# A vision tower on one core: gamma folded into a second out product, residual with row sums by VectorE, rests of B and C by TensorE, a third unit times B by GpSimd, steps re-placed

## What is computed

```
h = h + attn(layernorm(h))
attn(x):
    x_inner, z = split(x @ W_in)                      # 384 channels each
    x_conv = silu(conv4(x_inner) + conv_b)
    B, C  = split(x_conv @ W_x)                       # 16 states each
    delta = softplus(x_conv @ W_dt + b_dt)
    for t: s = exp(delta[t] * A) * s + delta[t] * x_conv[t] * B[t]
           y[t] = sum over states of s * C[t]
    y = (y + D * x_conv) * silu(z)
    out = y @ W_out
    return (out - mean(out)) / sqrt(var(out) + 1e-5) * gamma + beta
ffn: h = h + experts(layernorm(h))                    # router on layernorm(h), capacity, top 1
```

## Time and profile before

| | |
|---|---|
| median of 3 runs | 2686.87 us (2685.8 to 2687.75) |
| the profiled execution, its own time | 2688.49 us |
| span of its instructions | 2686.8 us |
| PE busy / weight loads | 2361.2 us (88%) / 1497.1 us |
| DVE busy | 2228.8 us (83%) |
| POOL busy | 2162.1 us (80%) |
| ACT busy | 2058.0 us (77%) |

### The profile page before, as it was taken

How to read it: one execution, slowest core, us unless ns; L and a number is a source line. 1 busy time by engine, 2 the same in 40 slices (tenths; PEclk the granted TensorE clock), 3 DMA queues, 4 the chain that set the end, 5 groups by cost and what they waited for, 6 DMA issues and landing times. The chain is left out here.

```text
span 2686.8 us, 37764 instructions
## 1 busy us (share of the span) xinstructions
PE 2361.2 (88%) x12483; PEld 1497.1 (56%) x12483; DVE 2228.8 (83%) x2304; ACT 2058.0 (77%) x4606; POOL 2162.1 (80%) x1004
## 2 busy tenths in 40 slices
PE   7798898988989988988989898998885479999997
PEld 4444555545555554555555455555442278888887
DVE  1799999999999999999999999999999885222222
ACT  2789988899999999899889999999986463333333
POOL 0599999999999999999999999999998314544432
PEclk9999999999999999999999999999986589999999
DMA  3445555555555555555555555555443035766654
GB/s 110 115 122 135 132 131 120 118 131 138 130 124 118 118 118 135 122 133 130 135 119 119 136 132 132 122 118 118 118 112 87 19 109 190 232 222 220 218 182 156
DMA packets 164569, 361.07 MB, mean 134 GB/s; under 512 B 17457, under 2 KB 88697, under 8 KB 156952
## 3 DMA queue, kind: packets, MB, share of 16 engines
q1 hardware_dynamic: 152504, 329.59, 48.6%
q0 software_dynamic: 11872, 29.07, 3.3%
HBM read 292.28 MB, written 68.52 MB: 134 GB/s over the span
## 5 line engine op out<-in xcount | busy, mean ns | idle before, releaser
L1600 DVE TENSOR_TENSOR_SCAN arena<-banks,arena 128x788 f32<-128x788 f32 x768 | 1339.9, 1778 | 1.4 <-ACT banks L733 1.0
L541 POOL TENSOR_TENSOR arena<-arena 128x1576 f32<-128x1576 f32 x384 | 1242.6, 3260 | 23.7 <-DVE arena L1600 22.9
L733 ACT ACTIVATE banks<-arena,neg_a 128x392 f32<-128x392 f32 x1536 | 839.1, 580 | 95.2 <-DVE arena L1600 84.6
L1589 DVE TENSOR_TENSOR arena<-arena,banks 128x1576 f32<-128x1576 f32 x320 | 565.7, 1768 | 24.5 <-PE banks L1130 14.5
L1146 PE MATMUL banks<-arena,gather_q 128*32 128x394 f32 x3072 | 341.8, 526 | 22.5 <-POOL arena L541 21.7
L1093 PE MATMUL banks<-arena,v_lo 128*128 128x394 f32 x768 | 293.2, 526 | 8.9 <-ACT arena L816 8.0
L1852 DVE TENSOR_TENSOR arena<-banks,arena 128x384 f32<-128x384 f32 (+1 forms) x57 | 30.2, 530 | 325.4 <-PE banks L1471 325.4
L693 POOL DMA_INDIRECT out_tokens<-arena x106 | 107.2, 1011 | 231.0 <-DVE arena L1867 207.3
L1072 PE MATMUL banks<-wtok,arena 128*99 128x192 f32 x1536 | 264.5, 329 | 13.9 <-DMA arena<-in_x 11.5
L1072 PEld LDWEIGHTS banks<-wtok,arena 128*99 128x99 f32 x1536 | 249.3, 167 | 35.9 <-issue 30.3
L1040 ACT ACTIVATE arena<-banks 128x256 f32<-128x256 f32 (+1 forms) x57 | 21.1, 370 | 281.9 <-PE banks L1437 281.9
(11 more groups left out here) (272 smaller groups left out, 4103.2 us busy)
## 6 DMA issues: line engine op xcount, KB each, us to landing
arena<-delta_du_scratch SPq DMA_DIRECT2D x384, 394.0 KB, 10.6
arena<-in_w_pack SPq DMA_DIRECT2D x57, 1155.0 KB, 5.3
delta_du_scratch<-arena SPq DMA_DIRECT2D x96, 394.0 KB, 3.5
arena<-in_x SPq DMA_DIRECT2D x32, 1176.0 KB, 10.5
rows_scratch<-arena SPq DMA_DIRECT2D x32, 297.0 KB
rows_scratch<-arena SPq DMA_DIRECT2D x32, 294.0 KB
arena<-in_b SPq DMA_DIRECT2D x57, 96.0 KB, 5.2
arena<-in_conv_w SPq DMA_DIRECT2D x1, 2304.0 KB, 11.0
```

What stands on the lines that cost most here:

```text
L541: pool.tensor_tensor(v[:, :, :], v[:, :, :], c_rep[(NG * n + u % NG) % CREPS].unsqueeze(1).to_broadcast([P, NQ, N2]), ALU.mult).then_inc(s ...
L733: ins = act.activation(o, d, ACT.Exp, scale=neg_a[:, c:c + 1])
L1589: dve.tensor_tensor(hb[(UNITS * n + u) % BUFS][:, :, :], rep[m][:, :, 1, :], ps_b[:, 0:N2].unsqueeze(1).to_broadcast([P, NQ, N2]), ALU.mul ...
L1600: dve.tensor_tensor_scan(v, decay[k % 2], v, 0.0, ALU.mult, ALU.add).then_inc(s_scan, 1)
```

## The change

1. **Gamma in a second out product.** `wog` is the centred out weights times gamma, made once by VectorE. `scaled_product` multiplies y by it; `out_product` stays, but only its squares are used, and ScalarE takes them straight from the bank (`out_squares`, now by halves b). `copy_out`, `out_norm` and `apply_gamma` go.
2. **Residual by VectorE.** `add_residual` (two halves of two instructions) computes bank x 1/deviation + (h + beta) and sums each row; ScalarE makes mean and squares of the rows (`row_squares`) in place of VectorE's statistics.
3. **Rests of B and C by TensorE.** `less_first` and `less_second` add minus identity times the bf16 part to the bank of the product; ScalarE copies the second and third part from that bank. `rest_bc` and `last_bc` go.
4. **Unit 1's product with B by GpSimd**: `BY_POOL = (1, 5, 9)`.
5. **Other places** for steps on all four engines, other bank numbers. Both token halves now use banks of one parity (`TOKS` 9 and 11), both halves of the front transposes do not (`FT` 19 and 20). In the last passes the two residual steps stand ahead of `weigh` and `choose` on VectorE.

```diff
-        BY_POOL = (5, 9)
+        BY_POOL = (1, 5, 9)
...
-        K_OF = (20, 1, 21, 12, 8, 7, 4, 15, 13, 14)
-        OUT, TOKS, FT = (5, 6), (9, 10), (17, 19)
-        BT, CS, ROUTE = (11, 16), (22, 0, 2, 3), 18
+        K_OF = (22, 1, 23, 21, 8, 5, 4, 16, 6, 14)
+        OUT, TOKS, FT = (2, 10), (9, 11), (19, 20)
+        BT, CS, ROUTE = (12, 15), (24, 0, 3, 7), 18
+        OUTG = (13, 17)
...
+            def out_squares(n, r, o, b):
+                act.wait_ge(s_opmm, 2 * n + b + 1)
...
+                for f in range(2):
+                    c = 2 * b + f
+                    ins = act.activation(rows[r][:, c, DIM:2 * DIM], kbank(OUT[b], o)[0:H0, f * DIM:(f + 1) * DIM], ACT.Square,
+                                         accum_out=sq2[:, c:c + 1])
+                ins.then_inc(s_osq, 1)
...
+            def less_first(n, r, o):
+                pe.wait_ge(s_gev, 10 * n + TAKEN[BC])
+                pe.matmul(kbank(K_OF[BC], o)[:, 0:N2], minus, bc3[r], start=False, stop=True,
+                          skip_group_check=True).then_inc(s_bcrest, 1)
...
+            def scaled_product(n, o, b):
...
+                v = kbank(OUTG[b], o)
+                for f in range(2):
+                    c = b * L + f * HSTEP
+                    for k in range(MB):
+                        mm = pe.matmul(v[0:H0, f * DIM:(f + 1) * DIM], y[:, k, c:c + H0], wog[:, k, :], start=(k == 0),
+                                       stop=(k == MB - 1))
+                mm.then_inc(s_ogmm, 1)
...
+            def add_residual(n, r, o, b):
+                dve.wait_ge(s_ogmm, 2 * n + b + 1)
...
+                for f in range(2):
+                    c = 2 * b + f
+                    ins = dve.scalar_tensor_tensor(out=rows[r][:, c, 0:DIM], in0=kbank(OUTG[b], o)[0:H0, f * DIM:(f + 1) * DIM],
+                                                   scalar=rs2[:, c:c + 1], in1=rows[r][:, c, 0:DIM], op0=ALU.mult, op1=ALU.add,
+                                                   accum_out=sum3[:, c:c + 1])
+                ins.then_inc(s_resid, 1)
...
+                    if 2 in on and u == 5:
+                        pe.wait_ge(s_h, 2 * (i + 2) + 1)
+                        tok(i + 2, r, 1)
...
+                    if 2 in on and u == 6:
+                        if -1 in on:
+                            pe.wait_ge(s_resid, 2 * (i - 1) + 2)
+                        else:
+                            pe.wait_ge(s_h, 2 * (i + 2) + 2)
+                        front_t(i + 2, r, 0)
```

More of the change, by code:

```diff
@@ L164, in build @@
         h2_hi = carve(P, 4, H0)
-        st1, st3 = (carve(H0, 4, 6) for _ in range(2))
-        mv1, mv3 = (carve(H0, 4, 2) for _ in range(2))
+        sum3, neg3, sq3, var3 = (carve(H0, 4) for _ in range(4))
         sq2, var2 = (carve(H0, 4) for _ in range(2))
@@ L637, in body @@
                 for u in range(UNITS):
-                    if -2 in on and u == 0:
-                        centre_rows(i - 2)
                     if 0 in on and u > 0:
@@ new lines, in body @@
+                    if 0 in on and u == 5:
+                        spread_b(i, r, 7)
+                    if 2 in on and u == 5:
+                        pe.wait_ge(s_h, 2 * (i + 2) + 1)
+                        tok(i + 2, r, 1)
+                    if -2 in on and u == 5:
+                        if i == PAIRS + 1:
+                            rank(FIRST, 1)
+                        if -1 in on:
+                            pe.wait_ge(s_osq, 2 * (i - 1) + 2)
+                        else:
+                            pe.wait_ge(s_resid, 2 * (i - 2) + 2)
+                        back_t(i - 2, r, r, 0)
@@ L1695, in body @@
                         take_y(i - 1, o, 2)
+                    if 0 in on and k == 3:
+                        bx(i, 2)
                     if 0 in on and k == 4:
```

523 lines of the change are left out of this document (246 added, 277 removed).

## The result

| | before | changed |
|---|---|---|
| median of 19 runs each, us | 2686.64 | 2691.7 |
| lowest to highest, us | 2684.79 to 2690.24 | 2686.47 to 2697.88 |
| ratio, 95% interval | | 1.0019, 1.0013 to 1.0025 |
| profiled execution, its span, us | 2688.49, 2686.8 | 2691.57, 2689.8 |

The changed kernel is slower by 0.19%, 5 us. The time lies in my range, but its sign is not the one that I gave most.

What follows compares the result with a forecast made beforehand. VectorE was the bound, GpSimd 2% behind; after the change a ring between them would set the pass. Loop -21.6, start +5.5 and end +12 sum to -4.1 us: 2683 us against a median of 2686.87, range 2648 to 2712.

Steps and rivals of the forecast that it cites:

- my range: Whole time, 2648 to 2712 us; chances were faster 0.46, same 0.22, slower 0.32.
- Slots: Instruction times in a pass, counted start to start, such as 1.70 us a scan; VectorE's work came to 59.6.
- The ring: Main loop: GpSimd's unit 1 product and VectorE's scans wait for each other, ScalarE's block between; closes at 61.9 us a pass.
- A: End of GpSimd's product with B for unit 1; 16.6 us to its unit 3 product with C, then 45.3.
- the wait at scan 6: VectorE at scan 6 waits for ScalarE's lengthened block at step 5, about 1.0 us in every pass.
- Rival (a): Main loop: scan 6 does not wait, pass 60.9 us, time 2652, half case 2667; chance 0.28.
- The loop: First product with B to last scan, 32 passes: -21.6 us, with 4.5 allowed for lower-clock stretches.
- rival (b): TensorE sets the pass, through its late half's front transposes and state sum: 62.7 us, time 2708; chance 0.27.
- The start: Up to the first product with B: second token half waits for the first's embedding, plus a z product; +5.5 us.
- The end: Last scan to last logits: weigh and choose wait behind the second residual step; 47.2 against 35.3 us, +12.
- the low half of the forecast: Part of the main forecast's 0.38 chance counted as faster: 0.14 below 2681.5 us.

Runs made afterwards that it cites:

- y_block: Changed kernel with ScalarE's two-part copy of the third delta block behind the decays of step 6 instead of ahead; ratio to the kernel before 1.0011.
- x_copyc: Changed kernel with ScalarE's fourth copy of C one step earlier, ahead of decays 8; ratio to the kernel before 1.0026.
- x_start: Changed kernel with the second pair's first token half embedded inside the first softplus, not behind it; ratio to the kernel before 0.9988.
- v_after: The changed kernel, unchanged, run again beside the kernel before on another chip; ratio 1.0020.
- x_end: Changed kernel with the router's weighing and choosing ahead of the last two residual steps; ratio to the kernel before 0.9991.
- z_se: Changed kernel with both edits outside the loop, earlier token embedding and earlier weighing and choosing; ratio to the kernel before 0.9963.

## Why the prediction was wrong

**Slots.** Right for scans, products and GpSimd. Two small things were missing from VectorE's work: a scan right behind the product that feeds it comes 1.88 after it, not 1.69 (1358.53 to 1360.41 against 1362.12 to 1363.81), twice a pass where the order before had none; and a residual step takes 0.41 us, a slot of 0.34, where I put 0.27. The four statistics I took off at 0.34 each, their length, where the earlier trace rows has four in 1.11, 0.24 less. VectorE's own slots came to 61.92 - 0.70 - 0.49 = 60.7, not 59.6; the three make 0.9 of this 1.1.

**The ring** came out at 61.92 for 61.9, with parts other than mine. From A (1352.04 and a slot of 2.94) to product 3 (1371.77) it took 16.8 for 16.6, the rest 45.1 for 45.3. But product 3 waited for ScalarE's fourth copy of C, behind decays 8, and not for scan 7: y_block and x_copyc show that the ring runs through ScalarE as far as the exponential, and the wait at scan 6 is a sign of this, not its price. I gave 1.0 to scan 6 and it was 0.5, as VectorE's 8.47 of filling was 8.8 with the slots above. That two errors cancelled is luck. Rival (a) had scan 6 not waiting, and it waited; y_block, which halved that wait, got 0.1 us off the pass, not the wait's size.

**The loop.** -13.0 for -21.6. The 31 passes hold 62.22 x 31 = 1928.9, and I had 31 x 61.9 + 4.5 = 1923.4, 5.5 us less: over 61.92 a pass the disturbances cost 9.4 us, not 4.5. The 0.5 us of slack that I had given VectorE's late half was not there, for TensorE's sum of unit 4 ended at the moment product 10 needed it (1396.3). This is rival (b)'s place, in 9 passes of 30 at 0.8 us each, so 7.5 us where (b) had 25. Its mechanism, a late sum behind a waiting transpose, is only half of it: the transposes wait 0.56 in the undisturbed passes too, and VectorE waits only where the lower clock comes on top. The other 3 us are in the first pass, where scan 2 waited 2.14 us for GpSimd's product 1 and scan 0 came 0.6 later than a slot behind its product, which I had not walked.

**The start.** +11.7 for +5.5, the largest miss, and outside even my bound of 9. The mechanism was right as far as it went (x_start): the second half waits for the first one's embedding. Its size was not. From the first embedding to the last is 7.0 us more than before, for 4: the products of the second half take 6.84, and 4.06 at the full clock. The first embedding came at 76.20 for 73.50, 2.7 for the 1.5 of the z product; in v_after, where the delta products ahead of it took 4.21 us instead of 5.90, it came at 74.44 and the first product with B at 99.8. The other 2.0 I had not seen: from the last embedding to the first product with B it is 18.5 us, 16.5 before, and x_start has the 18.5 as well. In the new order the B/C product and its two corrections stand behind the front transposes (92.50 us; before, it stood ahead of them at 74.75); no run looked at this alone.

**The end.** +8.3 for +12, mechanism right (x_end). I took the low-clock rate, 3.28 us for a half out product; they ran in 2.1 to 2.2, and the weighing started 20.2 behind the last scan, not 24.6; the wait for the rank products was 6.1, for 5. The sum as printed has 8.0 for the ranks, where the earlier trace rows gives 8.4; with that it comes to its 47.2.

**The rest** was 4.0 shorter on the profiled execution, which I had not forecast. All seven traces of changed kernels on the faster chips have 552 to 555 us, the one trace of the kernel before 558. No experiment looked at it, and its cause stays open; TensorE's wait for a transfer ahead of the experts' products, 2.6 us in that trace and at most 1.6 in these, covers a part.

**The verdict.** The three terms were of the right sign, and each difference of a few us decided: start and end cost 20.0 together where I had 17.5, and the loop gave 13.0 for 21.6. I called the likeliest single time a wash and still gave "faster" the largest chance, by rival (a) and the low half of the forecast. The steps that failed are two terms of the sum, both too favourable. The loop's -21.6 measured -13.0: the allowance for passes at the lower clock was half of what the disturbed passes cost, and the first pass was not walked. The start's +5.5 measured 11.7: about 4 of the 6 missing are TensorE's lower clock, 2 the B/C product behind the transposes.

## What to carry over

A re-placement that relieves the bound engine is worth what the ring that is next allows, so walk it through every engine, with the rows of work that run without a gap, and walk the first pass as well as a middle one; a wait that you can see marks a ring but isn't its price, and filling it with work from behind pushes something else late. Price the prologue and the epilogue of a software pipeline with the same care as a pass: here 32 passes gained 13 us and two places that run once lost 20, and two edits of a few lines there made the kernel 0.37% faster than before. Where TensorE's queue is in order, don't put a product that waits ahead of ones that don't.

## What the runs showed of the hardware

- TensorE's granted clock depends on placement enough to undo a change: one state sum moved ahead of the front transposes took the loop from 0.99 to 0.96 granted and 23 passes of 29 from 61.9 to 64.8 us (y_sum4), with nothing added; the six passes that kept the full rate took 62.0.
- A scan directly behind the VectorE product that it reads comes 0.19 us later than one behind other work (1.88 against 1.69).
- The same kernel takes 2687 us on two chips and 2709 to 2711 on three; in the changed kernel's variants the main loop's passes agreed to 0.1 us, and what differed was the part behind the last logits (552 to 555 against 573 to 581 us). In each run on the slower three, TensorE's expert products wait 2.7 to 14.5 us in all for a semaphore whose release the profile puts outside the core's engines ("remote"), on the faster two in none; and from 92 to 230 us behind the last logits its granted clock is 0.89 to 0.93 in z_se, 1.00 in the changed kernel. By the kernel's order this semaphore should be that of the experts' weights, which is inferred. The waits cover a part of the 20 us, and why they come is open.
